# A graph-attention layer on one core: every super's last tile fetched row by row, and the fp32 one-hot written by VectorE behind the merge

## The reference

```python
h = relu(layernorm(x)) @ W_node.T            # 4 heads of 32
att = leaky(sum(a * [h[src], h[dst], edge @ W_edge.T]))      # per edge and head
m = max(segment_max(att, dst), 0)
ex = exp(att - m[dst])
denom = segment_sum(ex, dst) + (num_edges - deg) * exp(-m)
out = x + segment_sum(ex / denom[dst] * h[src], dst)
```

## Time and profile before

| | |
|---|---|
| three runs | 2084.69, 2089.64, 2090.17 us |
| the profiled execution: time, span | 2090.56 us, 2088.7 us |
| busy: TensorE, VectorE, ScalarE, GpSimd | 1460.6, 1575.2, 768.6, 1542.5 us |
| mean granted TensorE clock | 0.63 of full |
| chain that ended last | GpSimd 54%, issue 22%, VectorE 8%, TensorE 8% |

### The profile page before, as it was taken

One profiled execution on the slowest core, in us unless ns is written; L12 is line 12 of the kernel. 1 busy time (PEld: TensorE's weight loads), 2 busy tenths in 40 slices (PEclk: granted clock), 3 DMA queues, 4 the chain that ended last, 5 costly groups with the idle time before them and its releaser, 6 DMA issues.

```text
span 2088.7 us, 46636 instructions
## 1 busy us (share of the span) xinstructions
PE 1460.6 (70%) x8371; PEld 1227.2 (59%) x8372; DVE 1575.2 (75%) x4485; ACT 768.6 (37%) x2304; POOL 1542.5 (74%) x1635
## 2 busy tenths in 40 slices
PE   6456867686867776676676676677677677677685
PEld 6445656565656555565565565566566565566564
DVE  8778888787886776776776786786776786786777
ACT  7733433333343243243243243243243243243333
POOL 7777777777777777777777777777777777777770
PEclk9756767666665666566655665555655555665656
DMA  9953344343343334334334334334334333334331
GB/s 277 311 151 109 97 114 116 95 117 93 97 117 104 101 96 111 91 96 112 91 96 112 92 95 112 92 96 111 92 96 110 93 96 111 92 96 110 92 94 29
DMA packets 131275, 230.42 MB, mean 110 GB/s; under 512 B 45539, under 2 KB 90231, under 8 KB 124215
## 3 DMA queue, kind: packets, MB, share of 16 engines
q0 software_dynamic: 51968, 109.76, 23.5%
q1 hardware_dynamic: 44075, 87.75, 12.9%
q10 hardware_dynamic: 34932, 30.38, 4.5%
HBM read 182.03 MB, written 45.71 MB: 109 GB/s over the span
## 4 chain that ended last, share of the span: by engine, by line
POOL 54%; issue 22%; DVE 8%; PE 8%; ACTq 2%; ACT 2%; DMA 1%; DVEq 1%; POOLq 1%; SPq 0%
POOL gath L578 54%; PE bank_rn L1416 3%; PE bank_p L1473 2%; PE bank_w L1473 2%; DVE bank_rn L868 1%; DVE vals L988 1%; ACTq L339 1%; DVE zz L619 1%; ACT gath L1149 1%; PE bank_rn L1424 1%; DMA resets<-ef 1%; ACTq L94 1%; DVEq L94 0%; DVE vals L627 0%; SPq L455 0%
## 5 line engine op out<-in xcount | busy, mean ns | idle before, releaser
L578 POOL DMA_INDIRECT gath<-h_table,idx x1576 | 1495.2, 949 | 484.5 <-issue 478.7
L1473 PEld LDWEIGHTS bank_p<-vals,onehot 128*128 128x128 f32 x1664 | 382.9, 331 | 89.9 <-DVE vals L988 50.7
L1473 PE MATMUL bank_p<-vals,onehot 128*128 128x137 f32 x1664 | 414.0, 442 | 2.6 <-DVE vals L988 2.3
L1263 ACT ACTIVATE ab<-ab_log 128x8 f32<-128x8 f32 x209 | 43.5, 208 | 943.8 <-DVE ab_log L915 832.7
L1473 PEld LDWEIGHTS bank_w<-vals,onehot 128*128 128x128 f32 x1664 | 326.4, 287 | 94.4 <-DVE vals L988 73.0
L1473 PE MATMUL bank_w<-vals,onehot 128*128 128x137 f32 x1664 | 354.2, 393 | 23.8 <-DVE vals L988 23.3
L1449 PE MATMUL bank_s<-s_live,onehot_bits 128*128 128x24 bf16 x1672 | 79.1, 181 | 358.6 <-ACT onehot_bits L1291 358.5
L1416 PEld LDWEIGHTS bank_rn<-w_edge_bd,ef 128*128 128x128 f32 x1664 | 300.0, 282 | 15.1 <-DMA ef<-in_edges 15.1
L1416 PE MATMUL bank_rn<-w_edge_bd,ef 128*128 128x8 f32 x1664 | 294.9, 319 | 14.8 <-DMA ef<-in_edges 14.8
L1449 PEld LDWEIGHTS bank_s<-s_live,onehot_bits 128*128 128x128 bf16 x1672 | 74.2, 109 | 384.8 <-ACT onehot_bits L1291 380.4
L880 DVE SCALAR_TENSOR_TENSOR onehot_bits<-bank_w,tables,zz 128x1024 bf16 (+1 forms) x209 | 268.3, 1284 | 24.1 <-issue 5.1
(11 more groups left out here) (189 smaller groups left out, 1637.3 us busy)
## 6 DMA issues: line engine op xcount, KB each, us to landing
ef<-in_edges SPq DMA_DIRECT2D x52, 1024.0 KB
gath<-h_table SPq DMA_DIRECT2D x3256, 0.5 KB
out_x<-x_all ACTq DMA_DIRECT2D x210, 128.0 KB
gath<-h_table,idx POOLq DMA_INDIRECT x1576
gath<-h_table ACTq DMA_DIRECT2D x1480, 0.5 KB
x_all<-in_x SPq DMA_DIRECT2D x14, 448.0 KB, 12.3
out_x<-x_all SPq DMA_DIRECT2D x14, 448.0 KB
h_table<-gath SPq DMA_DIRECT2D x11, 462.0 KB
```

The lines of the kernel that those rows point to most:

```text
L578: e.indirect_dma_start(gath[:, q * GPS + g, t * ROW:(t + 1) * ROW], None, table, bass.IndirectOffsetOnAxis(idx[:, q, g * TILES + t:g * TIL ...
L1473: ins = e.matmul(half_p[q], onehot[q][:, t, :], vals[q][:, t, :], start=(t == 0), stop=(t == TILES - 1))
```

## The change

1. **All supers by hand.** `HAND_QS` becomes `(0, 1, 2, 3)`: from super 3 on each of 49 supers has one tile fetched row by row. The 128 rows are split 28 + 28 + 24 on SyncE and 4 + 6 + 6 + 32 on ScalarE. ScalarE loads 4 offsets ahead of its first rows, 12 behind the first step's store, and 32 in the fourth step, right ahead of its 32 rows.
2. **The one-hot.** VectorE writes it in fp32 itself; ScalarE's widening copy is gone. It stands behind the merge, ahead of the rescale, and no longer ahead of the normalising. The addition to the output windows moves ahead of the product with the gathered rows.
3. **ScalarE's order.** Rows stay ahead of `factors`; the extra copies of the second and fourth step follow `factors`, then the store, then the 12 offsets.
4. **Prologue.** Seven of the 14 output pieces are copied after the first terms are loaded.

```diff
-HAND_QS = (1, 2, 3)
+HAND_QS = (0, 1, 2, 3)
-SP_PARTS, ACT_PARTS = (32, 28, 28), (8, 8, 8, 16)
+SP_PARTS, ACT_PARTS = (28, 28, 24), (4, 6, 6, 32)
+ACT_LOADS = (4, 12, 0, 32)
...
-                    wait(e, s_of, s)
-                    s_col = s + 3
-                    one_hot(1 - q, *((slot_b, off_b) if q == 0 else (slot_c, off_c)), s_col)
                     if q == 0:
                         slot_c, off_c, w_past0, w_past1, slot_d, off_d = load(
...
                     normalise(s, s_1)
+                    past_window((w_past0, w_past1)[q], s, s_1)
                     wait(e, s_ex, s_1)
...
                     merge(q, s, s_1)
-                    past_window((w_past0, w_past1)[q], s, s_1)
-
+
+                    s_col = s + 3
+                    one_hot(1 - q, *((slot_b, off_b) if q == 0 else (slot_c, off_c)), s_col)
                     rescale(q, s, s_1)
...
                     matched(s_2)
+                    if beside[q][1]:
+                        beside[q][1]()
+                    factors(s, s_1)
+                    if beside[q][0]:
+                        beside[q][0]()
+                    store((past_0, past_1)[q], s_1)
                     if beside[q][2]:
                         beside[q][2]()
-                    factors(s, s_1)
-                    widened(1 - q, s, s_2)
-                    if beside[q][0]:
-                        beside[q][0]()
-                    if beside[q][1]:
-                        beside[q][1]()
-                    store((past_0, past_1)[q], s_1)
...
+                def rows_ahead(k):
...
+                    if k in (0, 3):
+                        load_rows(k)
+                    at = sum(ACT_PARTS[:k])
+                    rows_by_hand(e, d_hand_act, next_q, SP_ROWS + at, offs[at:at + ACT_PARTS[k]])
...
+                def rows_behind(k):
+
+                    if by_hand and k == 0:
+                        load_rows(1)
+
+                def parts(k, extra=None):
+
+                    return extra, lambda: rows_ahead(k), lambda: rows_behind(k)
...
+                     (parts(0), parts(1, lambda: z_places(b, slot0)), parts(2), parts(3, step_3)))
```

More of the change, by code:

```diff
@@ L67 @@
 STAGED = 3
+FILLS_FIRST = CHUNKS // 2
 LAST_TILES = -(-(N_EDGES - (GROUPS - 1) * GROUP) // P)
@@ L150, in build @@
         bits_mem = sb("onehot_bits", [P, 3, TILES, P], BF16)
-        onehot_b = [bits_mem[:, i, :, :] for i in range(2)]
         onehot_t = bits_mem[:, 2, :, :]
@@ L332, in settle, with row_offsets, rows_by_hand @@
             e.sem_inc(passed, 1)
-        def rows_by_hand(e, landed, q, first, count):
-            offs = load(nc, e, hand_offs[0:1, q, first:first + count],
+        def row_offsets(e, q, first, count):
+            return load(nc, e, hand_offs[0:1, q, first:first + count],
                         [WINDOWS * P * ROW_BYTES - ROW_BYTES] * count)
+        def rows_by_hand(e, landed, q, first, offs):
             for k, off in enumerate(offs):
@@ L439, in _, with fill @@
                         ).then_inc(d_place_out, 16)
-            for c in range(CHUNKS):
-                e.dma_start(out[:, c * CHUNK:(c + 1) * CHUNK, :], x_all[:, c * CHUNK:(c + 1) * CHUNK, :]
-                            ).then_inc(d_fill, 16)
+            def fill(chunks):
+                for c in chunks:
+                    e.dma_start(out[:, c * CHUNK:(c + 1) * CHUNK, :],
+                                x_all[:, c * CHUNK:(c + 1) * CHUNK, :]).then_inc(d_fill, 16)
+            fill(range(FILLS_FIRST))
             e.wait_ge(d_place_out, 16)
@@ L467, in _ @@
                 load_terms(q, q)
+            fill(range(FILLS_FIRST, CHUNKS))
             def next_indices(b, q):
@@ L512, in feed @@
                     if by_hand:
-                        rows_by_hand(e, d_hand_sp, next_q, sum(SP_PARTS[:k]), rows)
+                        first = sum(SP_PARTS[:k])
+                        rows_by_hand(e, d_hand_sp, next_q, first, row_offsets(e, next_q, first, rows))
             next_edges(0)
@@ L880, in one_hot @@
                 e.scalar_tensor_tensor(
-                    out=onehot_b[buf][:, :, :],
+                    out=onehot[buf][:, :, :],
                     in0=ring_p[:, bass.ds(offset, P)].rearrange("p (a j) -> p a j", a=1)
@@ L1075, in _ @@
             off_0, _, slot_1, off_1 = load(nc, e, first_rec[0:1, :], [P, SPARE, SLOTS - 1, P])
+            wait(e, n_terms, TERMS + 2)
             one_hot(0, 0, off_0, 2)
@@ L1293, in matched @@
                     ).then_inc(s_e, 1)
[L1295 to L1298, removed]
             def feed(i, q, last_turn):
@@ L1308, in feed, with load_rows @@
                 next_i, next_q = (i, q + 1) if q + 1 < RING else (i + 1, 0)
-                def by_hand(k):
-                    if final or not handed(next_i, next_q):
+                by_hand = not final and handed(next_i, next_q)
+                offs = []
+                def load_rows(k):
+                    offs.extend(row_offsets(e, next_q, SP_ROWS + len(offs), ACT_LOADS[k]))
+                def rows_ahead(k):
+                    if not by_hand:
                         return
@@ L1330, in _ @@
             matched(1)
-            wait(e, s_oh, 1)
-            e.copy(onehot[0][:, :, :], onehot_b[0][:, :, :]).then_inc(s_of, 1)
             z_maxima(0, 0)
```

12 lines of the change are left out of this document (4 added, 8 removed).

## The result

The changed kernel takes **2165.91 us** (median of four runs, 2164.17 to 2168.14), the kernel before, run beside it, 2087.3 us. The ratio is **1.0372**, with a 95% interval from 1.0359 to 1.0385: slower by 3.7%. The forecast was 2166 us. The profiled execution took 2167.32 us for a span of 2165.5 us.

A forecast was written before the change was run, and what follows sets the result against it. GpSimd's gathers bound the kernel; after the change the walks' loop would: 192 + 49 x 39.3 = 2117.7, plus tail 46.6 and 1.9 around the span, gives 2166 us, range 2074 to 2205.

The forecast's parts named there:

- a super: One turn of the walks' loop in the changed kernel: 39.3 us, between 37.3 and 40.7, more than GpSimd's 38.8.
- The bound and the loops: GpSimd's gathers set the end before; the walks' loop catches up, and after the change sets the end itself.
- the walks' free pace: Walks' loop from super 2 to super 14, where VectorE does not wait for gathered rows: 34.1 us a super.
- slack: Room of the walks' loop: from 34.1 us a super up to 37.75, below which the change would be faster.
- The fourth step (+4.3): Fourth step's reduce to its rescale, which waits for `ab` behind ScalarE's 32 rows: 11.4 us becomes 15.7.
- The rest (-0.4, +0.6, +0.7): Rescale to the next fourth reduce, 22.7 us before: widening copy gone -0.4, third step +0.6, first step +0.7.
- uncovered register load: VectorE's first and third steps: register load loses the one-hot's cover, 1.2 to 1.5 us.
- window additions: VectorE's additions to the output windows, which now wait for `normed`: 0.15 us added.
- Prologue and tail: Walk 0 up to 2.7 us sooner, GpSimd's 3.60 us stop can shrink, `z_columns` of super 2 at 192; tail 46.6 us.
- Cover: SyncE's 80 rows take 33.5 us a super, leaving 5.3 of 38.8 us; GpSimd waits for `released`.
- GpSimd still sets the end: Rival, chance 0.15: the walks' loop stays under 37.5 us a super, giving 2077 us, faster.
- late stores: Rival, chance 0.07: window additions wait for stores behind 32 rows, 1 us more per super: 40.5 or more, 2225 us.

The follow-up runs named there:

- g2_after_fewer: The changed kernel with one more tile left out of GpSimd's gathers in each super with a tile, 49 supers: 2167.31 us.
- g3_before_fewer: The kernel before with one more tile left out of GpSimd's gathers in its 37 supers with a fetched tile: 2044.07 us, ratio 0.9793.
- f3_rows_only: The kernel before with the new rows alone (every super, 28, 28, 24 and 4, 6, 6, 32), its order kept: 2083.49 us, ratio 0.9985.
- f2_old_rows: The changed kernel with the old rows (three supers of four, 32, 28, 28 and 8, 8, 8, 16): 2094.51 us, ratio 1.0042.
- g1_regs: The changed kernel with VectorE's register load moved behind product L996 and the window additions behind the merge: 2096.6 us, ratio 1.0067.
- f1_spread: The changed kernel with ScalarE's 48 rows in parts of 8, 12, 12, 16 instead of 4, 6, 6, 32: 2079.42 us, ratio 0.9965.

## Why the prediction was right

| term | predicted | measured |
|---|---|---|
| 32 rows on ScalarE | 11.2 us | 11.10 |
| fourth reduce to the first row | 4.2 us | 1023.51 - 1019.50 = 4.0 |
| fourth reduce to the rescale | 15.7 us | 15.57 (49 supers) |
| rescale's wait for `ab` | 3.3 us | 151.1 / 48 = 3.15 |
| rescale to the next fourth reduce | 23.6 us | 23.74 |
| a super | 39.3 us | 39.31 |
| `z_columns` of super 2 | 192 us | 194.25 |
| tail | 46.6 us | 45.0 |
| time around the span | 1.9 us | 1.8 |

**The bound and the loops.** Right. That `z_columns` did not wait for rows in the first 14 supers showed the walks' free pace and the slack of 3.7 us, and g2_after_fewer and g3_before_fewer show that the end changed hands. The slack is that of the prediction, 37.75 - 34.1. The chain of the kernel before gives GpSimd and its gaps 76%; from these shares the change is a gain of 15 us.

**The fourth step (+4.3).** Right, at +4.21, and it was worked out from two rows of the trace. The prediction set against it the Trainium skill, page "DMA: Bandwidth & Descriptors", with some 50 ns of sequencer dispatch, given there for GpSimd's path; the estimate of 1.6 us for 32 rows that it made from this does not hold for ScalarE's rows, which took 11.10 us. The page's rule itself compares initiating a DMA with the DMA, and how long one of these rows is under way no trace here shows.

**The rest (-0.4, +0.6, +0.7).** Right in sum (+0.9, measured +1.0), less so in its parts. f3_rows_only shows that fewer rows in the first three steps gave back 0.7 us a super; VectorE's order cost 1.7. The prediction had both inside its +0.7 and +0.6, each smaller. Nor are these two numbers fixed prices: beside the old rows the same order cost 0.05 us of this term (f2_old_rows), which the prediction did not see. It took the uncovered register load for 1.2 to 1.5 us; in the third step it shows 0.9 us of idle where it showed 0.4 before. Its split by steps was better: the first took 7.60 us for 6.77 (+0.8), the third 7.82 for 7.85, where +0.6 was put. The window additions were counted with 0.15 us; g1_regs makes it likely that they cost the most. And the normalising was to start 3 us after the reduce in the first step; it starts 2.4 after it (1040.06, 1042.43).

**Prologue and tail.** Both off, against each other. The first walk was to begin up to 2.7 us sooner and GpSimd's stop to shrink; the stop grew from 3.60 to 7.42 us and `z_columns` of super 2 came 2.25 later than put. The tail grew by 1.6 us and not by 3.2. The stop is 6.14 us in f2_old_rows and 2.84 in f3_rows_only, so it grew with the new order or the new prologue and not with the rows; which of the two was not tried.

**The total.** 2165.91 us for a forecast of 2166 is closer than the terms are. That the loop was met within 0.01 us, though its steps were off by up to 0.6 us, and that prologue and tail cancel, is luck; 0.1 us in the loop is 5 us of time. The prediction's bounds for the loop do not follow from those of its terms either: these add up to 36.9 and 41.0 us, and it has 37.3 and 40.7. What was earned is the mechanism and the 15.7 us of the fourth step.

**Cover.** SyncE's 33.5 us were 32.3. GpSimd waits for released slots, 62.7 us in 101 waits (the four rows of that view that name L588 without "issue"), 7.4 of them the stop.

**Rivals.** "GpSimd still sets the end" fell with 39.31 us and g2_after_fewer; its price was right, as f1_spread (2079.42) shows, where it holds. The late stores are there: 65.6 us in 60 waits. But 47 us of them are in the fourth step, ahead of the wait for `ab`, where they cost nothing. The other 18 us, 0.4 us a super, are in the first step, ahead of no wait for `ab`; they are in the 39.31. The rival had the wait right, and missed that most of it is covered.

## What to carry to other kernels

When one engine's stream ends last and another loop catches up with it, look for the stretch in which the second does not wait: its pace there against the pace at the end is the slack, and a change to that loop is free up to it and counts once per turn beyond it. Two changes that each measure as nothing can then cost 3.7% together, so measure them in the regime in which they will run. And compare the period of the loop, step by step, not only the time: here it showed that three quarters of a loss that looked like used-up slack were the two changes lengthening the loop together. A list of small DMAs is work of the engine that issues it: put it where that engine's next result is not yet wanted, in portions no longer than the cover.

## What the runs showed of the hardware that was not expected

- **A queue of small DMAs can be held up on one chip and not on another.** 0.36 us a row on SyncE here, 0.73 us on the average on the first chip (51 rows in 37.21 us), with the same median of 241 ns for a row's own instruction and a longest of 1399 instead of 358 ns. The kernel before takes 3071 us there instead of 2087.
- **The same products run at either level of TensorE's clock.** The 32 products of the second step took 6.83 us at a granted clock of 0.50 (1.2 GHz) in the kernel before, and 3.90 us at 0.90 (most of it at 2.4 GHz) in f3_rows_only. The view by windows, of before and then of f3_rows_only: start and end, us, busy us of PE, PEld, DVE, ACT, POOL, clock, DMA share, GB/s.

```profile
1019.40:1026.30 6.90, 6.90 (x41) 6.90 (x40) 4.10 (x13) 2.44 (x6) 5.22 (x6) 0.50 0.33 80
```

```profile
1006.80:1010.80 4.00, 4.00 (x42) 4.00 (x40) 3.38 (x10) 1.93 (x7) 3.08 (x4) 0.90 0.37 95
```

  Of the 52 blocks 21 took under 5 us before, 37 in f3_rows_only and 33 in the changed kernel. The third step ends with these products, which is probably part of why f3_rows_only beat its expectation. Why the faster level is granted more often there was not tried.
- **A turn of the program's loop shows.** In one super of four the reduce behind the fourth step comes some 4 us later than in the others (5.0 instead of 1.0 to 1.3 us behind the rescale), in both kernels. What fills these 4 us is not known.
